# A four-layer sequence model: the D term moved into a TensorE accumulator, and three DRAM round trips replaced by on-chip buffers

## The reference, cut to what matters

```python
def _ssm(u, Wdbc, Wdt, bdt, Alog, Dp):
    dbc = einsum('bse,re->bsr', u, Wdbc)
    dlt, Bm, Cm = split(dbc, [R, R + N])
    delta = softplus(einsum('bsr,er->bse', dlt, Wdt) + bdt)
    dA, dBu = exp(delta[..., None] * -exp(Alog)), delta[..., None] * Bm[:, :, None, :] * u[..., None]
    # h = dA_t * h + dBu_t ; y = sum over n of h * C_t, for each of 256 steps
    return ys + u * Dp                      # the D term

x_ssm = ln(x) * (1 + scale) + shift         # skip = x_ssm
n = ln(x_ssm)
mz, mx = n @ Wz.T + bz, n @ Wx.T + bx
z1 = _ssm(mz @ Wc1.T + bc1, ...1)           # forward in time
z2 = flip(_ssm(flip(mz @ Wc2.T + bc2), ...2))
out = (silu(mx) * z1 + silu(mx) * z2) @ Wf.T + bf + skip
x = x + gate * out                          # then layer 3
```

## Time and profile before

| | |
|---|---|
| median of three runs | 5706.89 us |
| profiled execution | 5708.02 us, span 5706.3 us, mean granted TensorE clock 0.773 |
| VectorE (DVE) | busy 4861.3 us, 85% of the span |
| TensorE (PE) matmuls | busy 4166.5 us, 73% |
| ScalarE (ACT) | busy 3695.1 us, 65% |
| GpSimd (POOL) | busy 3172.3 us, 56% |
| DMA | 578.96 MB moved, mean 101 GB/s |
| chain that ended last | DVE 43%, PE 38%, issue 7%, POOL 4%, ACT 4% |

### The profile page before, as it was taken

The page is one execution under the profiler, slowest core; times in us unless marked ns, Lnnn a source line. Parts: engine busy times, 40 slices in busy tenths (PEclk is TensorE's granted clock), DMA queues, the critical chain, the costliest instruction groups (busy, mean ns, idle before and its releaser), DMA issues.

```text
span 5706.3 us, 69820 instructions
## 1 busy us (share of the span) xinstructions
PE 4166.5 (73%) x24852; PEld 2571.2 (45%) x24852; DVE 4861.3 (85%) x4908; ACT 3695.1 (65%) x8614; POOL 3172.3 (56%) x1452
## 2 busy tenths in 40 slices
PE   5667777778777777787777777777777777777644
PEld 4444444445444444444444444444444444444322
DVE  4228899998999989999999898999998998899896
ACT  0136676766667767666677666767766676677653
POOL 0015566656566655566666556666665566666564
PEclk7667777777878878778787778878877788778766
DMA  3013444443344444434444444344444434444441
GB/s 94 3 45 97 103 117 111 105 113 94 103 102 116 109 111 110 114 92 107 107 116 109 105 113 99 102 102 112 110 114 106 114 95 105 107 116 109 103 117 47
DMA packets 348556, 578.96 MB, mean 101 GB/s; under 512 B 58497, under 2 KB 151818, under 8 KB 340014
## 3 DMA queue, kind: packets, MB, share of 16 engines
q1 hardware_dynamic: 348206, 574.51, 39.7%
HBM read 436.93 MB, written 136.92 MB: 101 GB/s over the span
## 4 chain that ended last, share of the span: by engine, by line
DVE 43%; PE 38%; issue 7%; POOL 4%; ACT 4%; DVEq 0%; DMA 0%; SPq 0%; POOLq 0%; ACTq 0%
DVE S_X L714 20%; PE ps L164 20%; DVE ps L706 11%; PE ps L750 5%; PE ps L386 4%; PE ps L365 4%; POOL S_X L736 3%; DVE A_sm L422 2%; PE ps L154 2%; DVE A_raw L129 1%; PE ps L395 1%; ACT A_ring L147 1%; ACT A_ring L463 1%; PE ps L521 1%; DVE C_wa L562 1%
## 5 line engine op out<-in xcount | busy, mean ns | idle before, releaser
L736 POOL TENSOR_TENSOR S_X<-S_X,S_bc 128x1024 f32<-128x1024 f32 x1024 | 2411.9, 2355 | 1830.3 <-DVE ps L706 1830.1
L714 DVE TENSOR_TENSOR_SCAN S_X<-S_dA,ps 128x1024 f32<-128x1024 f32 x1024 | 2338.9, 2284 | 99.7 <-PE ps L750 5.9
L686 ACT ACTIVATE S_dA<-S_slot,acol 128x255 f32<-128x255 f32 x4096 | 1720.1, 497 | 628.2 <-DVE S_X L714 625.4
L706 DVE TENSOR_TENSOR ps<-S_slot,S_bc 128x1024 f32<-128x1024 f32 x1024 | 1311.9, 1281 | 27.0 <-DVE S_X L714 0.9
L750 PE MATMUL ps<-S_X,sum 128*32 128x256 f32 x8192 | 793.7, 493 | 641.0 <-POOL S_X L736 614.7
L750 PEld LDWEIGHTS ps<-S_X,sum 128*32 128x32 f32 x8192 | 219.0, 126 | 1024.5 <-POOL S_X L736 749.5
L365 PE MATMUL ps<-A_kP,A_qP 32*128 32x256 f32 x2048 | 394.9, 517 | 123.7 <-DVE A_sm L422 123.6
L154 PE MATMUL ps<-ident,A_ring 128*128 128x128 f32 x768 | 156.8, 339 | 401.8 <-ACT A_ring L147 302.1
L422 DVE TENSOR_REDUCE A_sm<-ps 128x4 f32<-128x1024 f32 x256 | 312.0, 1219 | 133.1 <-PE ps L365 133.0
L386 PE MATMUL ps<-A_qP,A_kP 32*128 32x256 f32 x2048 | 354.5, 472 | 64.8 <-ACT A_ring L463 53.2
L463 ACT ACTIVATE A_ring<-ps 128x1024 f32<-128x1024 f32 x256 | 260.6, 1018 | 179.3 <-PE ps L386 179.3
(11 more groups left out here) (312 smaller groups left out, 7270.8 us busy)
## 6 DMA issues: line engine op xcount, KB each, us to landing
S_slot<-scr_dd SPq DMA_DIRECT2D x1024, 256.0 KB, 4.9
scr_dd<-C_dd SPq DMA_DIRECT2D x64, 1024.0 KB, 4.8
S_bc<-scr_bc SPq DMA_DIRECT2D x256, 256.0 KB, 5.4
scr_wa<-C_wa SPq DMA_DIRECT2D x32, 1024.0 KB, 7.5
S_wa<-scr_wa SPq DMA_DIRECT2D x32, 1024.0 KB, 8.7
C_mod<-scr_mod SPq DMA_DIRECT2D x32, 512.0 KB, 9.5
scr_g<-S_g SPq DMA_DIRECT2D x32, 512.0 KB, 6.7
T_g<-scr_g SPq DMA_DIRECT2D x32, 512.0 KB
```

Of the source, the lines that this page charges most:

```text
L686: ins = a.activation(B["dA"][:, s, q % 2, j, lo:lo + T - 1], B["slot"][:, s, j, 0, lo:lo + T - 1], ACT.Exp, scale=K.k["acol"][:, s, 4 * c ...
L706: v.tensor_tensor(B["in"], B["slot"][:, s, :, 1, :], rep(B["bc"][:, s, q, :], 1, 4), ALU.mult).then_inc(S.dve.sem, 1)
L714: v.tensor_tensor_scan(line(X[:, u % 4]), line(B["dA"][:, s, q % 2]), line(B["in"]), 0.0, ALU.mult, ALU.add).then_inc(S.dve.sem, 1)
L736: g.tensor_tensor(B["X"][:, u % 4], B["X"][:, u % 4], rep(B["bc"][:, s, NQ + q, :], 1, 4), ALU.mult).then_inc(S.pool.sem, 1)
```

## The change

The D term is no longer made on DVE. In the setup, the two directions' folded weights are multiplied by D and summed into `wD` (128 x 2 x 512) and `bD`. Each quarter of S now starts with two matmuls that write wD times the normalised input into the accumulator (`proj`, first of them with start=True), and all `sum` matmuls of the quarter add to it. The steps `w0` and `w1` are gone. `g` and `gate` become one instruction: (PSUM + bD) * gate input. The gate inputs lie in K.wa with two buffers, S_g has two buffers, the residual K.xs has three, and C_xT has two (S reads it a turn later). The DRAM round trips of all three are gone with their DMAs: per batch three stores and three loads. T's own transposed input moves from C_xT to C_tmp. The order strings of all five queues are new. Diff (unchanged lines shortened; renamings left out):

```diff
@@ -101,14 +101,14 @@
-        dve += ["w" + s, "d" + s]
+        dve += ["d" + s]
...
-        dve += ["g%d" % ((v - 2) // 8), "gate%d" % ((v - 2) // 8)] if v >= 2 and (v - 2) % 8 == 7 else []
+        dve += ["gate%d" % ((v - 2) // 8)] if v >= 2 and (v - 2) % 8 == 7 else []
...
@@ -554,16 +552,6 @@
-        v.wait_ge(S.act.sem, S.act.at(b, "u1" + q))
-        if s:
-            v.wait_ge(S.dve.sem, S.dve.at(b, "w0"))
-        for c in range(KE):
-            if s == 0:
-                ins = v.tensor_scalar(B["wa"][:, c, 0, :], B["dd"][:, c, 1, :], k["dp"][:, 0, c:c + 1], None, ALU.mult)
-            else:
-                ins = v.scalar_tensor_tensor(B["wa"][:, c, 0, :], B["dd"][:, c, 1, :], k["dp"][:, 1, c:c + 1], B["wa"][:, c, 0, :], ALU.mult, ALU.add)
-        ins.then_inc(S.dve.sem, 1)
-        yield
         v.wait_ge(S.act.sem, S.act.at(b, "ln1" + q))
...
@@ -576,10 +564,13 @@
     a.wait_ge(S.pe.sem, S.pe.at(b, "xT"))
-    a.activation(flat(B["xT"]), bank[0][:, 0:512], ACT.Copy).then_inc(S.act.sem, 1)
+    if b >= 2:
+
+        a.wait_ge(K.S["S"].pe.sem, K.S["S"].pe.at(b - 2, "sum24"))
+    a.activation(B["xT"][:, b % 2].rearrange("p a b -> p (a b)"), bank[0][:, 0:512], ACT.Copy).then_inc(S.act.sem, 1)
...
@@ -617,14 +608,16 @@
         a.wait_ge(S.pe.sem, S.pe.at(b, "h%d" % h))
+        if h == 0 and b >= 2:
+            a.wait_ge(K.S["S"].dve.sem, K.S["S"].dve.at(b - 2, "gate3"))
         for c in range(2):
             f = 2 * h + c
-            ins = a.activation(B["wa"][:, f, 1, :], bank[h][:, c * T:(c + 1) * T], ACT.Identity, bias=k["bx"][:, f:f + 1])
+            ins = a.activation(K.wa[:, b % 2, f, :], bank[h][:, c * T:(c + 1) * T], ACT.Identity, bias=k["bx"][:, f:f + 1])
...
-    xs, mod, x = B["xs"], B["mod"], K.A["x"]
+    xs, mod, x, wa = K.xs[:, b % 3], B["mod"], K.A["x"], K.wa[:, b % 2]
     mo = lambda n: rep(mod[:, n, :], 1, TT)
     yield
     g.wait_ge(S.act.sem, S.act.at(b, "xn1"))
     g.wait_ge(K.land["mod"].sem, K.land["mod"].at(b))
-    if b:
-        g.wait_ge(K.land["res_out"].sem, K.land["res_out"].at(b - 1))
-    g.tensor_tensor(xs[:], B["xh"][:], mo(0), ALU.mult).then_inc(S.pool.sem, 1)
+    if b >= 3:
+        g.wait_ge(K.land["out"].sem, K.land["out"].at(b - 3))
+    g.tensor_tensor(xs, B["xh"][:], mo(0), ALU.mult).then_inc(S.pool.sem, 1)
     yield
...
@@ -717,13 +710,11 @@
             u, c = w - 2, (w - 2) // 8
             v.wait_ge(S.pe.sem, S.pe.at(b, "sum%d" % u))
             if c == 0:
-                v.wait_ge(K.land["wa"].sem, K.land["wa"].at(b))
-                if b:
-                    v.wait_ge(K.land["g_out"].sem, K.land["g_out"].at(b - 1))
-            v.tensor_tensor(B["g"][:, c, :], B["bank"][:, (c % 2) * T:(c % 2 + 1) * T], B["wa"][:, c, 0, :], ALU.add).then_inc(S.dve.sem, 1)
-            yield
-            v.wait_ge(S.dve.sem, S.dve.at(b, "g%d" % c))
-            v.tensor_tensor(B["g"][:, c, :], B["g"][:, c, :], B["wa"][:, c, 1, :], ALU.mult).then_inc(S.dve.sem, 1)
+                v.wait_ge(K.S["C"].pool.sem, K.S["C"].pool.at(b, "gate"))
+                if b >= 2:
+                    v.wait_ge(K.S["Tpe"].sem, K.S["Tpe"].at(b - 2, "wf"))
+            v.scalar_tensor_tensor(B["g"][:, b % 2, c, :], B["bank"][:, (c % 2) * T:(c % 2 + 1) * T], K.k["bD"][:, c:c + 1], K.wa[:, b % 2, c, :],
+                                   ALU.add, ALU.mult).then_inc(S.dve.sem, 1)
 
...
@@ -739,16 +730,23 @@
 def s_pe(p, K, b):
     S, B = K.S["S"], K.Sb
     for u in range(UNITS):
-        yield
         c, first, last = u // 8, u % 8 == 0, u % 8 == 7
+        if first:
+
+            yield
+            p.wait_ge(K.S["C"].act.sem, K.S["C"].act.at(b, "xT"))
+            if c:
+                p.wait_ge(S.dve.sem, S.dve.at(b, "gate%d" % (c - 1)))
+            elif b:
+                p.wait_ge(S.dve.sem, S.dve.at(b - 1, "gate3"))
+            for i in range(KD):
+                p.matmul(B["bank"][:, (c % 2) * T:(c % 2 + 1) * T], K.k["wD"][:, i, c * P:(c + 1) * P], K.C["xT"][:, b % 2, i, :],
+                         start=i == 0, stop=False, skip_group_check=True)
+        yield
         p.wait_ge(S.pool.sem, S.pool.at(b, "c%d" % u))
-        if first and c:
-            p.wait_ge(S.dve.sem, S.dve.at(b, "gate%d" % (c - 1)))
-        elif first and b:
-            p.wait_ge(S.dve.sem, S.dve.at(b - 1, "gate3"))
         for j in range(4):
             ins = p.matmul(B["bank"][32 * j:32 * j + 32, (c % 2) * T:(c % 2 + 1) * T], K.k["sum4"][:], B["X"][:, u % 4, j, :],
-                           start=first, stop=last, tile_position=(0, 32 * j), skip_group_check=True)
+                           start=False, stop=last, tile_position=(0, 32 * j), skip_group_check=True)
         ins.then_inc(S.pe.sem, 1)
...
@@ -760,9 +758,10 @@
     bk = B["bank"][0]
     yield
     p.wait_ge(K.land["t"].sem, K.land["t"].at(b))
+    p.wait_ge(K.S["S"].dve.sem, K.S["S"].dve.at(b, "gate3"))
     last_c(p, K, b)
     for t in range(TT):
-        ins = matmuls(p, bk[:, t * D:(t + 1) * D], [(B["g"][:, c, t * P:(t + 1) * P], k["wf"][:, c, :]) for c in range(KE)])
+        ins = matmuls(p, bk[:, t * D:(t + 1) * D], [(K.Sb["g"][:, b % 2, c, t * P:(t + 1) * P], k["wf"][:, c, :]) for c in range(KE)])
     ins.then_inc(K.S["Tpe"].sem, 1)
...
@@ -784,14 +783,15 @@
     v.wait_ge(S.sem, S.at(b, "gated"))
-    v.tensor_tensor(B["x"][:], B["x"][:], B["xh"][:], ALU.add).then_inc(S.sem, 1)
+    v.wait_ge(K.S["C"].pool.sem, K.S["C"].pool.at(b, "r3"))
+    v.tensor_tensor(x, x, B["xh"][:], ALU.add).then_inc(S.sem, 1)
     yield
...
@@ -837,11 +837,6 @@
-    yield
-    q.wait_ge(S.pool.sem, S.pool.at(b, "gate"))
-    q.wait_ge(S.dve.sem, S.dve.at(b, "w1"))
-    q.dma_start(K.scr["wa"][b], B["wa"][:]).then_inc(K.land["wa_out"].sem, 16)
-    q.dma_start(K.scr["res"][b], B["xs"][:]).then_inc(K.land["res_out"].sem, 16)
 
...
@@ -859,9 +854,6 @@
-    yield
-    q.wait_ge(S.dve.sem, S.dve.at(b, "gate3"))
-    q.dma_start(K.scr["g"][b], K.Sb["g"][:]).then_inc(K.land["g_out"].sem, 16)
 
...
@@ -881,32 +873,22 @@
-    yield
-    q.wait_ge(K.land["wa_out"].sem, K.land["wa_out"].at(b))
-    if b:
-        q.wait_ge(S.dve.sem, S.dve.at(b - 1, "gate3"))
-    q.dma_start(B["wa"][:], K.scr["wa"][b]).then_inc(K.land["wa"].sem, 16)
...
-    q.wait_ge(K.land["res_out"].sem, K.land["res_out"].at(b))
     if b:
-        q.wait_ge(K.land["out"].sem, K.land["out"].at(b - 1))
-    q.dma_start(B["x"][:], scr["res"][b]).then_inc(to, 16)
+        q.wait_ge(K.S["L3"].dve.sem, K.S["L3"].dve.at(b - 1, "x"))
     q.dma_start(B["gate"][:], scr["mod"][b][2].partition_broadcast(P)).then_inc(to, 16)
     q.dma_start(B["omL3"][PARTS:2 * PARTS, :], scr["mask"][b][2]).then_inc(to, 16)
     q.dma_start(B["pc"][:, 12:18], scr["pcol"][b][:, 12:18]).then_inc(to, 16)
-    yield
-    q.wait_ge(K.land["g_out"].sem, K.land["g_out"].at(b))
-    q.dma_start(B["g"][:], scr["g"][b]).then_inc(to, 16)
 
 
 def T_sp(q, K, b):
     yield
     q.wait_ge(K.S["L3"].dve.sem, K.S["L3"].dve.at(b, "x"))
-    q.dma_start(K.out[b].rearrange("(t p) d -> p t d", p=P), K.T["x"][:]).then_inc(K.land["out"].sem, 16)
+    q.dma_start(K.out[b].rearrange("(t p) d -> p t d", p=P), K.xs[:, b % 3]).then_inc(K.land["out"].sem, 16)
 
 
...
@@ -919,11 +901,11 @@
 }
 
 ORDER = {
-    "PE": "SASAASAAAASSCACSCCACCASSCASASAACCSSACCAACCAASSASASATAASSASTATASSATAAATSTSAASTATAATASSSASTASSTSAS",
-    "DVE": "SSSASSSCSSSAAASAAASCSSASASSSSSSCCAASSSSSSSSSSASASSSACCAASASASSSASSTASATSTSSSSSTSSTSSTSSTSTTSSSSSTSSTSSASASSASSSTASS",
-    "ACT": "SSSAASSCSAAAASACASCSCACCAAACASCCCCSAASSACSCSCSACCCCACSCCCSCCSSSASTTSAASATSATSATSAATSTASASATSTTTSATAAAA",
-    "Pool": "SSSSCCASCSCSCSASCSSSSSSCSCSSSSSSSSSTSSSSSTSAS",
-    "SP": "CSCtASCCStCSASSCsassTsSs",
+    "PE": "ASAAASASSACACASCSCASCCSSACSSAAASAAAASSASCCCACCASACSSAAAASSSTASSATAASATSASAATASAATTASATTSSSTATSSASSTS",
+    "DVE": "SASSSCSASASASAASCASSSSASASSSSSSSSAASSSSCSSASASASASSASSASCASASSASASSSSTTTSSSSSSTSTSSSTSSTSTSTSAAASTSSTSSSSSATS",
+    "ACT": "SSAASCSSAASAACASCASSCSACAACAASCSCCACACSASASSCSCCACSCCCCCCCCCSSSASSATASATSASATAASATASASTTTSASAAAATSTTTT",
+    "Pool": "SSCCSSASCSSSACSSCCSSSSSSSCCSSSSSSSSSTSSSSASTS",
+    "SP": "CtSSACSCSCCASSsasssT",
 }
...
@@ -1180,6 +1164,15 @@
+
+                v.wait_ge(spread, 16 * 2)
+                for i in range(KD):
+                    t.count(t.ready().tensor_tensor(M["wDs"][:, i, :] if s else k["wD"][:, i, :], k["wcz"][:, s, i, :], M["dprow" + q], ALU.mult))
+                    if s:
+                        t.count(t.ready().tensor_tensor(k["wD"][:, i, :], k["wD"][:, i, :], M["wDs"][:, i, :], ALU.add))
+                t.count(t.ready().tensor_tensor(M["bDs"][:] if s else k["bD"][:], k["bcz"][:, s, :], M["dp"][:, s, :], ALU.mult))
+                if s:
+                    t.count(t.ready().tensor_tensor(k["bD"][:], k["bD"][:], M["bDs"][:], ALU.add))
...
@@ -1327,6 +1320,10 @@
+            q.wait_ge(vector, mark["bz"])
+            for s in range(2):
```

(10 more changed lines are left out.)

81 lines of the change are left out of this document (40 added, 41 removed).

## The result

Four runs gave 5416.12, 5451.21, 5485.81 and 5577.43 us, median 5468.5, against 5707.9 for the kernel before; the ratio is 0.955 (95% interval 0.947 to 0.963), about 5451 us. Timed again, six runs gave a median of 5481.3 and a ratio of 0.9593 (0.9561 to 0.9624). Ratios leave out runs over 1.5% above the fastest of their kernel (5577.43 here), while medians in the text are of all runs. I forecast 5554 and a range of 5460 to 5645: the sign was right, the size was not. Runs of this kernel also differ far more than those of the kernel before, and that spread turned out to be part of the answer.

What follows compares the result with a forecast made beforehand. DVE was taken as the limit nearly everywhere, held up by PE in a few places. From 5708, -113 - 63 + 25 - 6 + 4 = -153 gave 5555 us, 5554 for the median; range 5460 to 5645, eight in ten.

Steps and rivals of the forecast that it cites:

- The orders: New order strings of all queues: costed at 0, bounds 87 us gained or the price of a longer end of turn.
- My own sign of being wrong: DVE's waits for PE grow by more than 2 us a turn, or fall by more than 3.
- The rival of closed gaps: New orders also close half of DVE's waits for maxima, gated and D sums: 87 us less, 5467 us; chance 0.13.
- D's term off DVE: w0 and w1 leave DVE, 3.64 us a turn, all of it counting in 31 turns: -113 us.
- Two operations into one: g and gate on DVE become one instruction of 416 ns, saving 1.98 us a turn: -63 us.
- The projection: Eight more PE matmuls, 3.2 us a turn; one quarter's 0.8 us charged as on the path: +25 us, bounds 0 and 102.
- The DRAM round trips: Six DMAs a batch go: worth nothing mid-run, 6 of 8 us at the run's end: -6 us.
- New waits: Waits on earlier turns' buffers cost 0; the close one, m1 behind the C_mod load, up to 1 us a turn (+31).
- Setup: Six 128x512 products or sums and four tiny ones on DVE before the bd copies: +4 us, bounds 0 and 6.
- The end of the turn becomes the bound: Rival: ACT's chain at turn's end makes DVE wait 11.8 us, against 4.5: 5787 us, slower; decides from 9.3; chance 0.08.
- What I left out: GpSimd's m1 and m2 could each hold up a DVE b product by 0.8 us, 51 us at most; not in sum.
- my 163.9: Length in us of a turn before the change, from 937 b products, 32 to a turn, between 704.7 and 5504 us.

Runs made afterwards that it cites:

- old_orders: Changed kernel with the five order strings of the kernel before, less the steps that are gone, each proj just ahead of its first sum: 5574.8 us, ratio 0.9761.
- no_proj: Changed kernel without the eight projection matmuls of a batch, so D times u is missing from the sums: 5461.1 us, ratio 0.9565.
- fill_light: Changed kernel plus idle matmuls: four ahead of layer 3's first transposes, one behind the scores of pairs 5 and 6: 5417.1 us, ratio 0.9482.
- fill_light_again: The changed kernel with the same six idle matmuls (four ahead of layer 3, two behind scores), timed again in more rounds: 5436.0 us, ratio 0.9517.
- the fillers: Kernels with added PE matmuls that nobody reads, placed in PE's gaps; on the changed kernel their medians run from 5417.1 to 5588.9 us.

## Why the prediction was right or wrong

- **The step that failed is "The orders. ... I cost it at 0."** They are worth 94 us. I named what they could close (maxima, `gated`, D sums, up to 87 us) and gave it 0.13. Measured from `old_orders` to the changed kernel, the waits for maxima fell from 91.9 to 33.1 us in 4400 us, layer 1's last sum from 70.9 to 4.6, the first gates from 28.5 to 3.9, while others rose (layer 3's last sum from 74.4 to 81.8, A_kP from 14.9 to 28.9). How much of it is gained depends on the clock: a turn with the new orders is 153.6 us when quick, 6.8 less than the 160.4 of the old ones, and up to 162.4 when slow, more than those. Times 28, 6.8 would be 190 us if every turn were quick. My own sign of being wrong, waits for PE that fall by more than 3 us a turn, came: 10.0 to 5.1.
- *The rival of closed gaps* said 5467, and the median of four runs is 5468.5. Its direction was right; that the number fits is luck. It had 2.7 us a turn of waits closed, where the orders closed 6.0 us of idle time and lost 3.3 to longer `b` products, and the single runs lie anywhere from 5416 to 5588.
- *D's term off DVE*, 3.64 us a turn: the instructions are gone and nothing took their place. With *two operations into one* and the projection it makes 133 us in `old_orders`, tail and setup included, where 153 was forecast for these; a turn fell by 4.1 us, and DVE's busy time by 5.0.
- *Two operations into one*: the gate takes 475 ns, not 416. I took the lower end of my bounds; the other, 479, the row of the same kind of instruction, was right. The saving is 1.74 us a turn, not 1.98: 8 us too much.
- *The projection* is mis-sized by reading a record for a matmul: the earlier trace rows are 464 matmuls in 236.4 us, 0.51 us each and 4.1 us a turn for eight. PE works 168.8 / 28 = 6.0 us a turn on it, not 3.2; that it is more than 4.1 goes with the clock, for half of its records (252 of 512) begin at the lower level and take 635 ns, the others 397. PE was to be busy 3 us more; it is busy 124.6 us a turn before and 119.5 now, at a clock of 0.86 instead of 0.79. The charge of 25 us stands against 3 to 20 in `no_proj`, which isn't clear of the spread: what the projection costs on the path stays open.
- *The DRAM round trips* of gate inputs and sums were worth nothing in the middle, as said. At the end `wf` starts 3.6 us after the last gate (7.0 before), now held by T_pc, where I took 2: the tail gained 3.4, not 6.
- *New waits*: GpSimd never waits for a DMA at `m1` in the 28 turns, so the close one cost nothing, as said.
- *Setup*: the six products and sums of 128x512 and three (not four) small ones are busy 4.7 us, forecast 4; the first `b` starts 5.2 us later (444.6 against 439.4).
- *The end of the turn becomes the bound*: no. Its waits fell from 4.5 to 86.4 / 28 = 3.1 us a turn. The 9.3 us from which it decides were never near; with L1.o first, A_x hardly waits, and layer 3's last sum waits 2.9 us.
- *What I left out*: the longer `b`. 32 x (1380 - 1281) = 3.2 us a turn, 100 us in the run, is the largest loss and was in no sum. It belongs to the new orders: with the old ones `b` takes 1276 ns, so their 94 us are what is left after it. The Trainium skill, "SBUF — State Buffer", "Who interferes with whom", has the mechanism, and the trace agrees: 2.30 us beside a GpSimd instruction of 1.26, 1.23 without. Where I applied it was wrong: m1 and m2 cost `b3` 0.4 us; `r1` and layer 1's product cost 1.1 each (`b6`, `b31`), layer 0's product 0.6 at `b9`, and `b10` and `b14` lose 0.6 and 1.0. Before, two products in a turn lost 0.8 each. The average rose, though GpSimd does the same work, since it matters beside what that work falls.
- A turn fell from 164.5 to 157.1 us (my 163.9 came from counting `b` in a stretch that was no whole number of turns). DVE's busy time fell by 149.1 - 146.7 = 2.4 us of that, not 5.5, and its idle time by 15.4 - 10.4 = 5.0. In two steps: removing the D term took 5.0 us of work away and left the idle time 1.0 higher, as my argument had it; the orders closed 6.0 us of idle time and cost 2.7 of work. What I argued holds for what I priced, and all of the closed time was in what I did not price.

Open: why a turn starts to be slow. Slow turns come in `fill_light` too, one of 160.5 us from 2544.9 us of the run on and three (159.2, 160.2, 154.5) from 4548.8 on; in `fill_light_again` four of them end by themselves. Two views go a step further than the waits above. The first is DVE in the turn from 2544.9, and in the turn ahead of 4548.8:

```profile
2548.95 2.29 DVE L714 TENSOR_TENSOR_SCAN S_X<-S_dA,ps 128x1024 f32<-128x1024 f32 x1 [0.48 <-DVE ps L706]
...
4484.59 1.23 DVE L706 TENSOR_TENSOR ps<-S_slot,S_bc 128x1024 f32<-128x1024 f32 x1 [0.46 <-DVE S_X L714]
```

These are gaps in which DVE waits for no other engine, 0.35 us longer than usual. There are five of them in the 28 turns, in the 11th, 13th (two), 15th and 25th, and the profiles of the changed kernel, its second timing and the fillers all have them at the same steps. In `fill_light` and `fill_light_again` slow turns begin in the 13th turn and in the 26th and nowhere else; the changed kernel's row of quick turns ends at the 26th too. The second view is the clock. The quick turn from 4395.0 and the slow one behind it, from 4548.8, are alike for 57 us, with 346 records of PE each, and then PE ends a gap of 4.91 us in both. The 8 us that begin inside that gap, in the quick turn and in the slow one:

```profile
4452.40:4460.40 8.00, 7.41 (x32) 6.14 (x33) 7.83 (x10) 5.59 (x16) 4.16 (x2) 0.79 0.50 144
...
4606.15:4614.15 8.00, 7.40 (x24) 5.86 (x25) 6.91 (x10) 5.59 (x16) 4.13 (x2) 0.59 0.51 151
```

So a shift of 0.35 us comes first, then the clock stays at its lower level for longer behind the same work, and only then does DVE wait. That the shift is the cause is likely by the places and not shown, for no run moved or made such a gap; what the gaps are, no view shows. That the slow turns lose their time in waits of DVE for PE, at the lower clock, is seen in the rows; that fillers change how often they come is shown; which gap of PE decides is not. The full change to on-chip buffers without the D term wasn't tried.

## What to carry to other kernels

An order written out for several engines is one object: price it by what each wait could become, give that rival real weight, and don't take the time of half an order for half its worth: here both halves cost more than the whole gained. Where PE has short gaps, look for more than one length of the same loop turn; if there are two, compare the granted clock in the same few microseconds of each, and try one or two idle matmuls in the gap before, since more can cost all that is gained. Before an instruction is priced from a group, count its records against the matmuls in the code, and take the row with the same operation even when another has the same operands.

## What the hardware showed that was not expected

A periodic program with constant work settles into different periods, 153.6 us or a cycle of turns from 154.8 to 162.4, and runs of one kernel spread by 3% (5416 to 5588 us) while the kernel before spread by 0.2%. Leaving work out (`no_proj`) moved the mean clock down (0.814 to 0.818, where eight of ten runs of the changed kernel have 0.833 to 0.850) and the time hardly at all. GpSimd and DVE exclude each other both ways. In the first two rows below, from the changed kernel, `m2` begins 0.47 us into a `b` and takes 2.12 us; in the last it begins with no `b` running and takes 1.28, as in all 13 such turns, against 2.12 in the 18 of the other kind. The waits of `c` for `b`, by far GpSimd's largest (1378.6 us in 28 turns), say nothing about this: in both kernels c of unit u has a wait for b of unit u+1 written in the program, so that the two mostly run one after the other.

```profile
3916.03 1.49 DVE L699 TENSOR_TENSOR ps<-S_slot,S_bc 128x1024 f32<-128x1024 f32 x1
3916.50 2.12 POOL L641 TENSOR_TENSOR xs<-xs,C_mod 128x512 f32<-128x512 f32 x1
...
5008.95 1.28 POOL L641 TENSOR_TENSOR xs<-xs,C_mod 128x512 f32<-128x512 f32 x1
```
